# Routing from the logits, weighing in five parts, and values made batch by batch in a twelve-stage network on one core

## What is computed

```python
def _L0_ffn_ref(x, Wg, bg, We, be):          # run twice, around the causal attention
    gate = jax.nn.softmax(x @ Wg + bg, axis=-1)              # 8 experts
    topk_vals, topk_idx = jax.lax.top_k(gate, 2)
    gate_sparse = (topk_vals placed at topk_idx) / their sum
    y = jnp.einsum('bsi,eoi->bseo', x, We) + be
    return jnp.einsum('bseo,bse->bso', y, gate_sparse)

def _L0_attn_ref(x, w_qkv, w_out):           # 16 heads of 8, rotated q and k, causal softmax over 256
    ...
def _L1_ffn_ref(x, router_w, ...):           # run twice: 16 experts, capacity 640 each, top 2
    logits = x_tokens @ router_w + router_b
    probs = jax.nn.softmax(logits, axis=-1)
    vals, idx = jax.lax.top_k(probs, 2)
    vals = vals / (jnp.sum(vals, axis=-1, keepdims=True) + 1e-09)
    pos = place of each choice in its expert's queue     # cumsum over the choices
    ...                                                  # experts, and a shared expert for all
def _L3_attn_ref(x, Wqkv, Wout):             # softmax inside blocks of 32 tokens only
    att = einsum(q, k) * scale; att = where(causal, att, min); att = softmax(att); out = einsum(att, v)
    return out @ Wout.T
```

## Time and profile before

| what | value |
|---|---|
| median of 3 runs | 3461.79 us (3454.87 to 3462.9) |
| the profiled execution | 3459.31 us, span 3458.0 us |
| busy in the span | PE 2666.1 us (77%), PEld 2086.4 (60%), DVE 2140.8 (62%), ACT 1787.5 (52%), POOL 1146.9 (33%) |
| mean granted clock of TensorE | 0.857 of 2.4 GHz |

### The profile page before, as it was taken

One profiled execution on the slowest core, in us unless ns is written; L12 is line 12 of the kernel. 1 busy time (PEld: TensorE's weight loads), 2 busy tenths in 40 slices (PEclk: granted clock), 3 DMA queues, 4 the chain that ended last, 5 costly groups with the idle time before them and its releaser, 6 DMA issues. The chain is left out here.

```text
span 3458.0 us, 67775 instructions
## 1 busy us (share of the span) xinstructions
PE 2666.1 (77%) x25429; PEld 2086.4 (60%) x25429; DVE 2140.8 (62%) x7889; ACT 1787.5 (52%) x3476; POOL 1146.9 (33%) x1567
## 2 busy tenths in 40 slices
PE   6788887649589568348678999999999855944775
PEld 3466664337367446235467888888888744633554
DVE  6566656773346743554377777777777765456456
ACT  5344435324235224225458998889989733621432
POOL 3200003450543430765563222222222236564002
PEclk9699988879779779568789999999999976975787
DMA  9300000015100025114300000000000001520000
GB/s 276 92 3 3 3 2 1 13 37 151 55 20 9 25 68 149 44 42 142 109 25 7 12 12 12 1 12 12 1 12 1 1 14 47 165 76 22 2 2 26
DMA packets 134055, 147.95 MB, mean 43 GB/s; under 512 B 14818, under 2 KB 109923, under 8 KB 133731
## 3 DMA queue, kind: packets, MB, share of 16 engines
q1 hardware_dynamic: 106306, 71.13, 7.0%
...
## 5 line engine op out<-in xcount | busy, mean ns | idle before, releaser
L203 PE MATMUL banks<-ident,xn 128*128 128x128 f32 x320 | 72.1, 366 | 326.9 <-DVE xn L191 211.4
L3054 POOL TENSOR_SCALAR shared_floats<-shared_floats 128x2 f32<-128x2 f32 x256 | 57.6, 225 | 715.1 <-DVE shared_floats L3045 714.5
L2976 PE MATMUL banks<-layer,shared_floats 128*128 128x128 f32 x2048 | 275.1, 278 | 0.0
L3287 ACT ACTIVATE shared_floats<-banks,layer 128x256 f32<-128x256 f32 x512 | 210.3, 472 | 90.4 <-PE banks L2963 90.3
L203 PEld LDWEIGHTS banks<-ident,xn 128*128 128x128 f32 x320 | 47.3, 184 | 346.2 <-DVE xn L191 216.0
L2976 PEld LDWEIGHTS banks<-layer,shared_floats 128*128 128x128 f32 x2048 | 253.4, 195 | 0.0
L2963 PE MATMUL banks<-shared_floats,layer 128*128 128x256 f32 x1024 | 243.1, 380 | 0.0
L3066 DVE TENSOR_SCALAR shared_floats<-banks,shared_floats 128x128 f32<-128x128 f32 x512 | 186.5, 406 | 57.9 <-POOL shared_floats L3056 57.8
L1266 POOL DMA_INDIRECT results<-results,result_rows x128 | 123.9, 968 | 257.6 <-DVE result_rows L1275 110.3
L3042 DVE BATCH_NORM_STATS2 shared_floats<-banks 128x6 f32<-128x128 f32 x512 | 126.3, 289 | 128.5 <-PE banks L2976 124.9
L2963 PEld LDWEIGHTS banks<-shared_floats,layer 128*128 128x128 f32 x1024 | 185.5, 191 | 20.1
...
## 6 DMA issues: line engine op xcount, KB each, us to landing
...
bins<-xn,f_bin_row POOLq DMA_INDIRECT x256
results<-results,result_rows POOLq DMA_INDIRECT x128
```

What stands on the lines that cost most here:

```text
L2976: m = T.matmul(to, hidden[:, n * S + t * P:n * S + (t + 1) * P], w["w2"][:, tile(n)], start=False, stop=(n == NF - 1), skip_group_check=True)
L3287: m = A.activation(hidden[:, n * S:(n + 1) * S], k.bank[5 + half][:, part], ACT.Gelu, bias=w["c1"][:, n:n + 1])
```

## The change

**The routers of ffn0 and ffn1.** The two largest are found on the logits and no longer on the softmax (both have the same order). `route_by_logits` takes MAX8 of the logits, whose first entry is the maximum that is subtracted; the exponential is then taken in place in `probs`. In ffn0 `router_pick` follows at once, and the weights are the exponentials at the chosen places over their sum. In ffn1 the picking and the cast of the choice stand before the layer norm of the next chunk, and `top_weights` makes the two weights of a token from the exponentials of the two largest logits, 8 more columns of the same `ACT.Exp`; `choose_rows` no longer makes them.

**The weighing of att0.** The job is now `("weigh", (rd, begin, end), behind)`: round 1 as one block and two, round 2 whole, round 0 as one block and one. The list is written anew; `project` 0, `heads` 0, `values` 2 and the turn of the next chunk move up as well.

**att3.** An even batch makes quarters 0 and 1 of the values, an odd one quarters 2 and 3, in banks 1 and 0 alternately; quarter 2 waits for the rotation of the next chunk's keys, since their projection lies in the same banks. On TensorE the result of the batch before is turned before the exponentials are; the output product comes before the second projection. On ScalarE the copy of the turned result stands before the copy of the turned exponentials, and the masking of the heads before the values. On VectorE the sum into x moves before the rotation in even batches and before the layer norm in odd ones.

```diff
--- before.py
+++ after.py
@@ -222,7 +222,8 @@
 def router_buffers(k, p, E, slot=0):
...
-    buffers = {n: k.sb(f"{p}_{name}", [P, TPC * most])[:, 0:TPC * E] for n, name in names.items()}
+    wide = {"probs": TPC * most + 2 * TPC if p == "f1" else TPC * most}
+    buffers = {n: k.sb(f"{p}_{name}", [P, wide.get(n, TPC * most)])[:, 0:TPC * E] for n, name in names.items()}
     buffers["hots"] = k.sb(f"{p}_hots", [P, 2 * TPC * most])[:, 0:2 * TPC * E]
@@ -258,6 +259,58 @@
+def route_by_logits(k, p, E, n, bias, slot=0):
+    V, b = k.nc.vector, router_buffers(k, p, E, slot)
+    logits, probs, top = b["logits"], b["probs"], k.sb("top", [P, TPC * 8])
+    first = top[:, :].rearrange("p (t k) -> p t k", k=8)[:, :, 0]
+    V.wait_ge(k.sem(f"{p}_logits"), n + 1)
+    k.v.count(V.tensor_tensor(by_expert(logits[:, :], E), by_expert(k.bank[1][:, 0:TPC * E], E),
+                              bias.unsqueeze(1).broadcast_to([P, TPC, E]), ALU.add))
+    V.wait_ge(k.v.sem, k.v.n)
+    for t in range(TPC):
+        k.v.count(V.max(top[:, t * 8:t * 8 + 8], logits[:, t * E:t * E + E]))
+    V.wait_ge(k.v.sem, k.v.n)
+    if p == "f1":
+        both = k.sb("top", [P, TPC * 8])[:, :].rearrange("p (t k) -> p t k", k=8)[:, :, 0:2]
+        k.v.count(V.tensor_tensor(top_exps(k).rearrange("p (t k) -> p t k", k=2), both,
+                                  first.unsqueeze(2).broadcast_to([P, TPC, 2]), ALU.subtract))
+        V.wait_ge(k.v.sem, k.v.n)
+    V.tensor_tensor(by_expert(probs[:, :], E), by_expert(logits[:, :], E),
+                    first.unsqueeze(2).broadcast_to([P, TPC, E]), ALU.subtract).then_inc(k.sem(f"{p}_shifted"), 1)
+
+def top_exps(k):
+    return k.sb("f1_probs0", [P, TPC * E1 + 2 * TPC])[:, TPC * E1:TPC * E1 + 2 * TPC]
+
+def exp_shifted(k, p, E, n, slot=0):
+    A, b = k.nc.scalar, router_buffers(k, p, E, slot)
+    to = k.sb("f1_probs0", [P, TPC * E1 + 2 * TPC])[:, :] if p == "f1" else b["probs"][:, :]
+    A.wait_ge(k.sem(f"{p}_shifted"), n + 1)
+    A.activation(to, to, ACT.Exp).then_inc(k.sem(f"{p}_exps"), 1)
+
+def top_weights(k, n, eps):
+    V, v = k.nc.vector, k.v
+    row_sum, exps = k.sb("row_sum", [P, TPC]), top_exps(k).rearrange("p (t k) -> p k t", k=2)
+    weight = routed(k, n)[0].rearrange("p (k t) -> p k t", k=2)
+    V.wait_ge(k.sem("f1_exps"), n + 1)
+    v.count(V.tensor_reduce(row_sum[:, :], by_expert(k.sb("f1_probs0", [P, TPC * E1 + 2 * TPC])[:, 0:TPC * E1], E1), AX.X, ALU.add))
+    for choice in range(2):
+        V.wait_ge(v.sem, v.n)
+        v.count(V.scalar_tensor_tensor(out=row_sum[:, :], in0=row_sum[:, :], scalar=1.0 if choice else eps, in1=exps[:, choice, :],
+                                       op0=ALU.mult, op1=ALU.add))
+    V.wait_ge(v.sem, v.n)
+    v.count(V.reciprocal(row_sum[:, :], row_sum[:, :]))
+    V.wait_ge(v.sem, v.n)
+    v.count(V.tensor_tensor(weight, exps, row_sum[:, :].unsqueeze(1).broadcast_to([P, 2, TPC]), ALU.mult))
 def router_choose(k, p, E, n, choice_bias=None, slot=0):
@@ -529,8 +582,9 @@
     def route(i):
...
-        router_shift(k, "f0", E0, n, k.w["L0_bg"][:, :], n % 2)
-        router_choose(k, "f0", E0, n, None, n % 2)
+        route_by_logits(k, "f0", E0, n, k.w["L0_bg"][:, :], n % 2)
+        router_pick(k, "f0", E0, router_buffers(k, "f0", E0, n % 2)["logits"], n % 2)
+        V.wait_ge(k.sem("f0_exps"), n + 1)
         normalised_weights(k, "f0", E0, 0.0, n % 2).then_inc(k.sem("f0_weights"), 1)
     def combine(i, first):
@@ -620,14 +674,14 @@
-    router_exp(k, "f0", E0, s.c0, s.c0 % 2)
+    exp_shifted(k, "f0", E0, s.c0, s.c0 % 2)
     ln_copy(k, s, 1)
...
-            router_exp(k, "f0", E0, n + 1, (n + 1) % 2)
+            exp_shifted(k, "f0", E0, n + 1, (n + 1) % 2)
         if i + 2 < NC:
@@ -942,12 +996,12 @@
     def route(i):
...
-        router_shift(k, "f1", E1, n, k.w["L1_router_b"][:, :])
+        route_by_logits(k, "f1", E1, n, k.w["L1_router_b"][:, :])
+        router_pick(k, "f1", E1, b["logits"])
+        V.tensor_copy(chosen_bf[:, :], b["hot"][:, :]).then_inc(k.sem("f1_chosen"), 1)
         if i + 1 < NC:
...
-        router_choose(k, "f1", E1, n)
-        V.tensor_copy(chosen_bf[:, :], b["hot"][:, :]).then_inc(k.sem("f1_chosen"), 1)
-        v.count(normalised_weights(k, "f1", E1, 1e-9))
+        top_weights(k, n, 1e-9)
     def place(i):
@@ -997,18 +1051,17 @@
-    counts, probs, product = k.sb("f1_counts", [P, TPC * E1]), b["probs"], k.sb("f1_product", [P, 2 * TPC * E1])
+    counts, product = k.sb("f1_counts", [P, TPC * E1]), k.sb("f1_product", [P, 2 * TPC * E1])
     place, within, spare = (k.sb(f"f1_{x}", [P, K1]) for x in ("place", "within", "spare"))
...
-    for values, to in ((probs[:, :], weight), (counts[:, :], place[:, :])):
-        v.count(V.tensor_tensor(both(product[:, :]), both(b["hots"][:, :]),
-                                values.unsqueeze(1).broadcast_to([P, 2, TPC * E1]), ALU.mult))
-        V.wait_ge(v.sem, v.n)
-        v.count(V.tensor_reduce(to, by_expert(product[:, :], E1), AX.X, ALU.add))
-        V.wait_ge(v.sem, v.n)
+    v.count(V.tensor_tensor(both(product[:, :]), both(b["hots"][:, :]),
+                            counts[:, :].unsqueeze(1).broadcast_to([P, 2, TPC * E1]), ALU.mult))
+    V.wait_ge(v.sem, v.n)
+    v.count(V.tensor_reduce(place[:, :], by_expert(product[:, :], E1), AX.X, ALU.add))
+    V.wait_ge(v.sem, v.n)
     v.count(V.tensor_scalar(within[:, :], place[:, :], float(CAPACITY), None, ALU.is_lt))
@@ -1033,7 +1086,7 @@
-    router_exp(k, "f1", E1, s.c0)
+    exp_shifted(k, "f1", E1, s.c0)
     ln_copy(k, s, 1)
@@ -1044,7 +1097,7 @@
-            router_exp(k, "f1", E1, n + 1)
+            exp_shifted(k, "f1", E1, n + 1)
         if i + 2 < NC:
@@ -1825,15 +1878,19 @@
-    def weigh(n, rd):
+    def weigh(n, part):
+        rd, begin, end = part
         v_heads = att_buffers(k, n // 2)[4]
-        to, at = k.bank[3], 0
-        if rd == 0:
+        to, blocks = k.bank[3], a.rounds_b[rd]
+        at = sum(last - first for _, first, last in blocks[:begin])
+        if rd == 0 and begin == 0:
             T.wait_ge(k.sem("at_v_heads"), 4 * (a.c0 + n // 2) + 4)
...
-        T.wait_ge(k.sem("at_exps"), a.u0 + n * a.units + 4 * rd + 4)
-        for b, first, last in a.rounds_b[rd]:
+        if begin == 0:
+            T.wait_ge(k.sem("at_exps"), a.u0 + n * a.units + 4 * rd + 4)
+        for b, first, last in blocks[begin:end]:
             blk, width = n % 2 * BLOCKS + b, last - first
@@ -1844,7 +1901,8 @@
-        m.then_inc(k.sem("at_weighed"), 1)
+        if end == len(blocks):
+            m.then_inc(k.sem("at_weighed"), 1)
     def turn_shifts(n):
@@ -2083,14 +2141,13 @@
-CAUSAL_ORDER = [("score", 0, 0), ("parts", 0, 1), ("values", 0, 0), ("copy values", 0, 0),
-                ("score", 1, 0), ("stats", 0, 0), ("weigh", 1, 2), ("shifts", 0, 1), ("copy shifts", 0, 1), ("project", 0, 0),
-                ("heads", 0, 0),
-                ("score", 2, 0), ("apply", 0, 0), ("values", 1, 0), ("copy values", 1, 0),
-                ("score", 3, 0), ("weigh", 2, 2), ("divide", 0, 2), ("project", 1, 0),
-                ("score", 4, 0), ("heads", 1, 0), ("out", 0, 2), ("values", 2, 0), ("copy values", 2, 0), ("turn", 0, 0),
-                ("copy turned", 0, 0), ("q heads", 0, 0), ("k heads", 0, 0),
-                ("score", 5, 0), ("add", 0, 2), ("weigh", 0, 1), ("values", 3, 0), ("copy values", 3, 0)]
+CAUSAL_ORDER = [("score", 0, 0), ("parts", 0, 1), ("weigh", (1, 0, 1), 2), ("values", 0, 0), ("copy values", 0, 0), ("project", 0, 0),
+                ("score", 1, 0), ("stats", 0, 0), ("heads", 0, 0), ("weigh", (1, 1, 3), 2), ("shifts", 0, 1), ("copy shifts", 0, 1),
+                ("score", 2, 0), ("apply", 0, 0), ("weigh", (2, 0, 3), 2), ("values", 1, 0), ("copy values", 1, 0),
+                ("score", 3, 0), ("divide", 0, 2), ("values", 2, 0), ("copy values", 2, 0), ("project", 1, 0), ("heads", 1, 0),
+                ("turn", 0, 0), ("copy turned", 0, 0), ("q heads", 0, 0),
+                ("score", 4, 0), ("weigh", (0, 0, 1), 1), ("out", 0, 2), ("k heads", 0, 0),
+                ("score", 5, 0), ("add", 0, 2), ("weigh", (0, 1, 2), 1), ("values", 3, 0), ("copy values", 3, 0)]
 CAUSAL = Softmax("L0_wqkvT", CAUSAL_A, CAUSAL_B, 8, 2, CAUSAL_ORDER)
@@ -2152,10 +2209,10 @@
+        else:
+            T.wait_ge(k.sem("at_qk"), LEFT["at_qk"] + 2 * c + 1)
             if c:
...
-        else:
-            T.wait_ge(k.sem("at_qk"), LEFT["at_qk"] + 2 * c + 1)
         for part in range(2):
@@ -2165,11 +2222,13 @@
-        if 4 * c + quarter:
-            T.wait_ge(k.sem("at_v_heads"), LEFT["at_v_heads"] + 4 * c + quarter)
+        if quarter == 2 and c + 1 < NC:
+            T.wait_ge(k.sem("at_qk"), LEFT["at_qk"] + 2 * c + 3)
+        elif quarter >= 2:
+            T.wait_ge(k.sem("at_v_heads"), LEFT["at_v_heads"] + 4 * c + quarter - 1)
         for b in range(4 * quarter, 4 * quarter + 4):
...
```

(50 more changed lines are left out.)

## The result

The changed kernel takes **3360.22 us**, the median of four runs (3356.96 to 3361.2), and the kernel before 3462.35 in four runs beside it: a ratio of 0.9699, with a 95% interval of 0.9667 to 0.973. It is faster by more than forecast: 3393 was predicted, with 3362 as the low end. The profiled execution took 3360.2 us for a span of 3358.8.

The account below looks back on a forecast made before the run. Each stage was taken as bound by its own loop: VectorE's routing, the routed chunk's period, TensorE's waits and low clock in both attentions. Terms -32 + 15 - 24 - 28 = -69 gave 3390, as median 3393 us, range 3362 to 3430.

Parts of the forecast that it names:

- L278, 0.76 here, where the like L325 takes 0.19: First feed-forward routing: this operation leaves VectorE's path, helping save 1.18 to 1.75 us a routing; 1.4 taken.
- +15: Routed feed-forward of 16 experts: the later layer norm costs about +7.5 us a stage, +15 for both; bounds 0 to +20.
- the 8.61 us start there: 16 experts: TensorE's turn, narrowing and counts wait for the later layer norm, then take 8.61 us; net +1.5 a chunk.
- first and last chunks give back: 16 experts' stages: first and last chunks give back 0.5 to 0.9 us each against the longer inner chunks.
- Rival B: 16 experts: the loop is not lengthened, about -3 us in place of +15, total 3375 us; chance 0.13.
- The walk: Causal attention: TensorE's list laid against VectorE's in the new order gives 18.6 us an even batch, 20.8 an odd one.
- The gap of 1.7 is longer than the 1.42 that has a low clock behind it today, so I leave one low stretch a pair: Causal odd batch: the wait before scoring 5 keeps a 1.7 us low-clock loss, so 22.5 us against 24.4.
- with one low stretch (1.7) 21.5: Blocked attention: a pair walked at 19.8 us, plus one low-clock loss, takes 21.5 against 25.6, saving 4.1.
- ScalarE copies the turned result before the turned exponentials: Blocked attention: with this copy order the output product finds its input ready, so its 2.31 us wait goes.
- A: All stages: TensorE's clock stays as it is, so the change gives only -37, 3425 us; chance 0.2.
- D: Blocked stage only: pieces are issued earlier but their data isn't there, so waits only move; 3421 us; chance 0.07.
- C: Causal stage: the clock falls for good, +190 us in seven pairs, total 3607 us; chance 0.05.

Follow-up runs that it names:

- att3_turned_last: Changed kernel, but in the blocked attention the result is turned and copied behind the turned exponentials; 3259.3 us, with 3347.4 for the kernel before beside it.

## Why the prediction was right or wrong

**First feed-forward: right in sum, wrong in its make-up.** Forecast -32, measured -29.6. The drops of the clock are gone (1.00 and 0.95; the second stage only begins at the low clock). But the period is 11.1 us in most chunks, not 10.3 to 10.7, and the routing takes 4.26 us at this place, not 3.3. Over all 16 routings the way from L245 (now L271) to the end of L325 (now L378) fell from 4.96 to 3.78 us, so 16 x 1.18 = 19 of the 22 us came, which is the lower bound. VectorE's timeline, after:

```profile
72.91 0.18 DVE L271 TENSOR_TENSOR shared_floats<-banks,L_bg 128x32 f32<-128x32 f32 x1
...
73.53 0.58 DVE L282 TENSOR_TENSOR shared_floats<-shared_floats,top 128x32 f32<-128x32 f32 x1
...
74.94 0.69 DVE L357 TENSOR_TENSOR shared_floats<-expert_ids,indexf 128x64 f32<-128x64 f32 x1
75.66 0.62 DVE L361 TENSOR_TENSOR shared_floats<-shared_floats 128x32 f32<-128x32 f32 x1
...
76.97 0.19 DVE L378 TENSOR_TENSOR shared_floats<-shared_floats,row_sum 128x32 f32<-128x32 f32 x1
```

and GpSimd's:

```profile
73.34 0.72 POOL L705 TENSOR_TENSOR shared_floats<-shared_floats 128x256 f32<-128x256 f32 x1
74.14 0.72 POOL L707 TENSOR_TENSOR shared_floats<-shared_floats 128x256 f32<-128x256 f32 x1
74.82 0.73 POOL L704 TENSOR_TENSOR shared_floats<-shared_floats 128x256 f32<-128x256 f32 x1
```

The step that failed is "L278, 0.76 here, where the like L325 takes 0.19". The forecast took 1.4 us a routing, with part of the 0.57 on top as gone; at this place it is 0.94 (5.20 to 4.26). The 0.57 was not L278's own: it is a wait for GpSimd's operation beside it, and it moved on to L357 and L361, whose likes took 0.23 and 0.19 in the chunk of the earlier trace rows. Both now end 0.05 to 0.08 us after an operation of GpSimd does (75.63 after 75.55, 76.28 after 76.23, where L705 runs once more). L361 takes 0.19 at 513.33 in the same kernel, with no GpSimd operation beside it. The Trainium skill says so ("SBUF — State Buffer", section "SBUF: two separate sides"): a VectorE operation with two SBUF inputs and a GpSimd operation take turns on one pair of ports. The trace agrees: L271, which reads PSUM and one SBUF input, keeps its 0.18 us.

**16 experts: +4, not +15; that the token stages alone gave +14.5 is luck.** L191 ends 3.86 us after the bias is added, as forecast (632.17 to 636.03). The period went to 15.45, not 16.2: the step that failed is "the 8.61 us start there". From L191's end to L1009 it is 7.83 us now. That stretch was not TensorE's work and its order, but ended with the hold of its signals, which hangs on the sends; VectorE goes on 11.7 us after the rows are written in both kernels (709.42 to 721.14 and 630.82 to 642.52). The earlier trace rows had the sign of it, "remote" before L955, and the prediction passed over it. Where nothing is held the cost is 13.7 - 12.5 = 1.2 us a chunk, near the 1.5 forecast.

The +14.5 is not that term either. From the first L955 or L1009 to the last the first token stage takes 100.3 us in both kernels: the first five periods are longer now and the last two shorter (14.1 and 8.7, against 14.7 and 11.7). Its 7.1 us come at the end, where the last shared sum waits for the sends:

```profile
714.35 0.69 DVE L1041 TENSOR_TENSOR shared_floats<-banks,xn 128x512 f32<-128x512 f32 x1 [10.91 <-remote]
```

And the stage behind gave most of it back, of which the prediction had only "first and last chunks give back": it starts from GpSimd's last send, which did not move (128.9 and 128.3). So the term is +4. Rival B had this doubt and the better number (-3).

**Causal stage: -34.2, not -24.** The walk was right: 18.6 and 20.8 by hand, 18.6 and 20.5 measured. The step that failed is "The gap of 1.7 is longer than the 1.42 that has a low clock behind it today, so I leave one low stretch a pair". The gap came out at 1.23, and the old odd batch had a second, longer wait of 1.81 us, with a low stretch of its own, which I had not put in the rows. That the clock fell behind the 1.42 was read rightly; whether it would have without the 1.81 was not tested. A pair takes 39.1 us where 41.1 was forecast, but the seven are 7 us shorter than forecast and not 14, since the first still begins at the low clock (280.2 us, not 7 x 39.1 = 273.7); the other 3 of the 10 us lie outside the seven pairs.

**Blocked stage: -42.2, not -28.** The step that failed is "with one low stretch (1.7) 21.5": none came in the inner pairs (clock 1.00), and a pair took 20.6 us where 21.5 was forecast and 19.8 walked. And the gain was counted for seven pairs where eight run: 8 x 5.0 = 40. The reason given for the 2.31 us ("ScalarE copies the turned result before the turned exponentials") was the smaller part: by att3_turned_last it gives 8.5 of the 42 us, and the rest of the stage's change, the values by batch above all, gives 34.

**The rivals.** A, the clock stays: wrong in all stages. The rule of the Trainium skill that it rested on ("TensorE: Matmul & The Clock Gate", "A second HAM failure mode: psum-queue depth-cycling") tells of a kernel of another kind and is not borne out here: seven causal pairs went at a clock of 0.98 and the blocked pairs at 1.00 while both change banks all the time and wait up to 1.23 us. D and C: wrong, nothing only moved and no clock fell for good.

The sum: the two attention terms were 24 us short, the routed one 11 us too dear, the first feed-forward 2 too good, all else +3: 69 + 24 + 11 - 2 - 3 = 99.
